# Preparation merged into the first attention: normalising, splitting and storing each pair of tiles while units run

## The reference

```python
x = x + _L0_xattn_ref(_layernorm(x, axis=-1), ctx_2048, ctx_2048)
# _L0_xattn_ref: 8 heads, each over 8 of the 64 rows of a batch
qk = jnp.einsum('bdm,bdn->bmn', qh, kh) * scale      # 256 x 256 for each head
sm = jax.nn.softmax(qk, axis=-1)
ret = jnp.einsum('bmn,bcn->bcm', sm, vh)
# _L3_xattn_ref: a decayed scan over the 64 context rows of a batch, then a mean over the rows,
# which the kernel folds into one weighted sum of the context's rows for each batch
```

## Time and profile before

| | |
|---|---|
| median of three runs | 2031.86 us (2029.39 to 2032.33) |
| span of the profiled execution | 2031.3 us; no other time is shown of that execution |
| busy: PE, DVE, ACT, POOL | 1408.2, 1363.5, 1120.5, 497.0 us |
| mean granted TensorE clock | 0.846 of full |
| preparation | 0 to 115.6 us (last store issued), first instruction behind the barrier at 118.9 |
| first attention | 118.9 to 579.2 us, with 64 units of about 6.3 us |
| DMA queue of SP | 116.46 MB, 23.0% of 16 engines' span |

### The profile page before, as it was taken

The page is one execution under the profiler, slowest core; times in us unless marked ns, Lnnn a source line. Parts: engine busy times, 40 slices in busy tenths (PEclk is TensorE's granted clock), DMA queues, the critical chain, the costliest instruction groups (busy, mean ns, idle before and its releaser), DMA issues. The chain is left out here.

```text
span 2031.3 us, 33248 instructions
## 1 busy us (share of the span) xinstructions
PE 1408.2 (69%) x11186; PEld 870.4 (43%) x11186; DVE 1363.5 (67%) x2850; ACT 1120.5 (55%) x1552; POOL 497.0 (24%) x903
## 2 busy tenths in 40 slices
PE   4429999999929894999626667379999646674111
PEld 4305555555527771555411333246565423342100
DVE  6646888888634534588867999535555468875896
ACT  4516777777712222677637888633434237875554
POOL 4411233333320004111013343200101001112663
PEclk9999999999959996999855766689999958877555
DMA  5652555555330003233110000011010120000111
GB/s 168 204 131 54 123 131 132 131 129 131 87 86 1 0 1 59 49 73 76 33 67 0 0 1 1 16 42 43 22 41 22 34 87 1 0 1 11 42 52 42
DMA packets 96387, 117.99 MB, mean 58 GB/s; under 512 B 29728, under 2 KB 82152, under 8 KB 91660
## 3 DMA queue, kind: packets, MB, share of 16 engines
q1 hardware_dynamic: 96268, 116.46, 23.0%
HBM read 80.07 MB, written 22.88 MB: 51 GB/s over the span
## 5 line engine op out<-in xcount | busy, mean ns | idle before, releaser
L610 DVE TENSOR_REDUCE ratt_nmax<-ratt_psS 128x2 f32<-128x512 f32 x512 | 318.7, 684 | 100.3 <-PE ratt_psS L502 98.7
L576 ACT ACTIVATE ratt_E<-ratt_psT 128x1024 f32<-128x1024 f32 x256 | 255.1, 1023 | 111.7 <-PE ratt_psT L524 111.6
L502 PE MATMUL ratt_psS<-ratt_K,ratt_Q 72*128 72x256 bf16 x1024 | 205.0, 285 | 42.9 <-DMA ratt_K<-context_parts 37.7
L524 PE MATMUL ratt_psT<-ratt_Q,ratt_K 75*128 75x256 bf16 x1024 | 196.8, 276 | 7.6 <-DMA ratt_Q<-ratt_rows 7.2
L502 PEld LDWEIGHTS ratt_psS<-ratt_K,ratt_Q 72*128 72x128 bf16 x1024 | 80.3, 99 | 139.5 <-issue 67.5
L537 PE MATMUL ratt_psO<-ratt_E,ratt_V 128*32 128x256 f32 x2048 | 138.8, 389 | 0.7 <-ACT ratt_E L576 0.7
L524 PEld LDWEIGHTS ratt_psT<-ratt_Q,ratt_K 75*128 75x128 bf16 x1024 | 99.9, 99 | 25.8 <-DMA ratt_Q<-ratt_rows 7.7
L3393 PE MATMUL final_psT<-final_identh,final_Z 128*128 128x128 f16 x64 | 8.3, 311 | 110.2 <-ACT final_Z L3427 110.2
L2195 PE MATMUL nffn_psH<-nffn_W,nffn_QT 128*128 128x512 bf16 x128 | 56.2, 589 | 28.8 <-ACT nffn_H L2274 19.9
L537 PEld LDWEIGHTS ratt_psO<-ratt_E,ratt_V 128*32 128x32 f32 x2048 | 53.8, 110 | 50.9 <-issue 28.1
L892 ACT COPY sffn_XS<-sffn_psG 128x512 f32<-128x512 f32 x8 | 4.7, 586 | 124.0 <-PE sffn_psG L841 124.0
(11 more groups left out here) (472 smaller groups left out, 3703.4 us busy)
## 6 DMA issues: line engine op xcount, KB each, us to landing
ratt_Q<-z_parts SPq DMA_DIRECT2D x32, 576.0 KB
ratt_K<-context_parts SPq DMA_DIRECT2D x96, 192.0 KB
gatt_V<-in_ctx_dram SPq DMA_DIRECT2D x16, 512.0 KB, 6.3
z_parts<-prep_ZS SPq DMA_DIRECT2D x48, 128.0 KB, 2.6
context_parts<-prep_CS SPq DMA_DIRECT2D x48, 128.0 KB, 2.3
head_sums<-ratt_O SPq DMA_DIRECT2D x64, 72.0 KB
all_X<-in_x_dram SPq DMA_DIRECT2D x8, 512.0 KB
prep_C<-in_ctx_dram SPq DMA_DIRECT2D x8, 512.0 KB
```

The source lines that it names most:

```text
L502: mm = nc.tensor.matmul(psS[:, RING[h], c * D:(c + 1) * D], Q9[0:R, buf, h, k % 2, c * P:(c + 1) * P], K9[0:R, buf, h, k % 2, :], start=Tr ...
L524: mm = nc.tensor.matmul(psT[:, p % 2, e, c, :], K9[0:RM, buf, h, u, c * P:(c + 1) * P], Q9[0:RM, buf, h, u, :], start=True, stop=True)
L576: nc.scalar.activation(E[:, 2 * b + p // 2, 2 * (p % 2):2 * (p % 2) + 2], psT[:, p % 2], ACT.Exp, scale=SCALE).then_inc(exped, 1)
L610: nc.vector.tensor_reduce(nmax[:, k % 2, h, :], psS[:, RING[h]].rearrange("p (c t) -> p c t", c=2), AX.X, ALU.max, negate=True).then_inc(m ...
```

## The change

Each engine does its steps of preparation at the end of its slot, behind everything of the units; the exceptions are `turn_context` on TensorE and `take_context` on ScalarE, which stand at the end of step p = 1:

```diff
+                # SP, behind bring_row, load_q or load_k, inverses_out, out, sums_back, back
+                    if at(n, 0) is not None:
+                        load_x(at(n, 0))
+                        load_c(at(n, 0))
+                    for part in range(3):
+                        if at(n, 3 + part) is not None:
+                            store_c(at(n, 3 + part), part)
+                        if at(n, 6 + part) is not None:
+                            store_z(at(n, 6 + part), part)
+                # load_q(g): sp.wait_ge(z_out, pair * 48 + 48); load_k(g): sp.wait_ge(c_out, pair * 48 + 48)
+                # TensorE, at the end of step p = 1
+                        if p == 1 and at(n, 1) is not None:
+                            turn_context(at(n, 1))
+                def turn_context(a):
+                    j = job["turn", a]
+                    pe.wait_ge(c_in[a % 2], a // 2 * 16 + 16)
+                    if j > 1:
+                        pe.wait_ge(exped, j - 1)
+                    for k in range(KC):
+                        for t in range(2):
+                            mm = nc.tensor.transpose(psT[:, j % 2, 0, k, t * P:(t + 1) * P],
+                                                     C[:, a % 2, t, k * P:(k + 1) * P], ident[:])
+                # ScalarE, behind the four exponentials (take_context at p = 1)
+                    if at(n, 2) is not None:
+                        first_of_c(at(n, 2))      # waits c_in, c_out of the pair before; copy to bf16
+                    if at(n, 4) is not None:
+                        normalise(at(n, 4))       # 2 activations, 128x256
+                    if at(n, 5) is not None:
+                        first_of_z(at(n, 5))      # waits z_out of the pair before; copy to bf16
+                # GpSimd, behind take, split_max, scale_and_add
+                    if at(n, 2) is not None:
+                        rest_of_c(at(n, 2))       # waits c_first of the same slot; subtract, 128x512
+                    if at(n, 3) is not None:
+                        root(at(n, 3))            # 4 small operations
+                        second_of_c(at(n, 3))     # copy to bf16, 128x512
+                    if at(n, 4) is not None:
+                        third_of_c(at(n, 4))      # subtract, 128x512
+                        weigh(at(n, 4))           # CT times the weights' row, 128x512
+                    if at(n, 6) is not None:
+                        rest_of_z(at(n, 6))       # subtract and copy to bf16, 128x512
+                    if at(n, 7) is not None:
+                        third_of_z(at(n, 7))      # subtract, 128x512
+                # VectorE, behind the maxima: take_stats (r = 1), aggregate (r = 2), sum_context (r = 6)
```

More of the change, by code:

```diff
@@ L427, in _ @@
[L427 to L434 removed]
+                        to = o_dram.rearrange("a (w g) c m -> a g c w m", g=4)[a, g]
@@ L475, in slot @@
-                def slot(i, k):
-                    n = i * 8 + k
+                    to = X[:, 2 * a:2 * a + 2, :]
+                    gp.tensor_tensor(to, to, num[:, a % 2], ALU.add).then_inc(added, 1)
+                for n in range(-LEAD, UNITS + 14):
                     if is_unit(n - LAG):
-                        take(i, k - LAG)
+                        take(n - LAG)
                     if is_unit(n - 1):
-                        split_max(n - 1, (k - 1) % 2)
-                    c = (k - 17) // 4
-                    if k % 4 == 1 and is_pair(i * 2 + c):
-                        scale_and_add(i * 2 + c, c % 2, i + c // 2)
@@ L485, in _ @@
-                slots(pool, slot, UNITS + 14)
+                        split_max(n - 1)
+                    if n % 4 == 1 and is_pair(n // 4 - 4):
+                        scale_and_add(n // 4 - 4)
+                    if at(n, 2) is not None:
[6 more added lines that the diff above has]
+                        weigh(at(n, 4))
@@ L562, in _ @@
-                slots(pe, slot, UNITS + LAG + 1)
+                            turn_max(n - 1)
             @block.scalar
             def _(act):
-                def row(u, b, half):
-                    act.wait_ge(turned, u + 1)
-                    if past(u, 2):
-                        act.wait_ge(row_in[b], half * 32)
-                    nc.scalar.copy(rows[:, b, :], psM[0:6 * NH0]).then_inc(row_out, 1)
-                def exp(m, b, p):
-                    act.wait_ge(shifted, m * 4 + (p + 1))
-                    if p == 0 and past(m, 2):
-                        act.wait_ge(pv, m - 1)
-                    nc.scalar.activation(E[:, 2 * b + p // 2, 2 * (p % 2):2 * (p % 2) + 2], psT[:, p % 2], ACT.Exp,
-                                         scale=SCALE).then_inc(exped, 1)
@@ new lines, in first_of_z, with first_of_c @@
+                def first_of_z(a):
+                    act.wait_ge(z_done, a * 2 + 2)
+                    if a > 0:
+                        act.wait_ge(z_out, a * 48)
+                    sc.copy(ZS[:, 0], Z[:]).then_inc(z_first, 1)
+                def first_of_c(a):
+                    act.wait_ge(c_in[a % 2], a // 2 * 16 + 16)
+                    if a > 0:
+                        act.wait_ge(c_out, a * 48)
+                    sc.copy(CS[:, 0], C[:, a % 2]).then_inc(c_first, 1)
+                act.wait_ge(decay_in, 16)
@@ L589, in slot @@
+                sc.activation(keep[:, 0:1], decay[:], ACT.Exp, scale=-1.0).then_inc(expd, 1)
+                for n in range(-LEAD, UNITS + LAG + 1):
                     m = n - LAG
@@ L613, in slot @@
[L613 to L622 removed]
+                            maximum(n, h)
```

683 lines of the change are left out of this document (322 added, 361 removed).

## The result

| | before | after |
|---|---|---|
| median of 4 runs | 2030.62 us (2029.39 to 2032.33) | 2093.69 us (2087.70 to 2094.44) |
| ratio to before | | 1.0307, 95% interval 1.0291 to 1.0323 |
| profiled execution, span | 2031.3 us | 2091.3 us (the run took 2093.05) |
| mean granted TensorE clock | 0.846 | 0.807 |
| copy of the row of unit 3, 8, 48, 63 (ACT) | 172.98, 203.75, 455.52, 549.66 | 68.36, 125.85, 504.51, 605.12 |

The account below looks back on a forecast made before the run. It took PE to be full (97.9 of 100 us) in the even attention, with no other engine near its limit. Span 2031.3 - 101 (front) + 129 (added to the slots) = 2059, so 2060 us, range 1992 to 2102.

Parts of the forecast that it names:

- The front: Start of the attention: first score at 40.5 us, slot 3 at 56 instead of 156.67, a gain of 101 us.
- The wait for C: TensorE's transposes wait for C, loaded too late in SP's queue: 5.9 us (4.9 to 7.8) per four slots.
- the list of the pairs: Which pairs wait for C: 5 to 15 in full, 11 times; pair 4 about 2 us; pair 3 none.
- GpSimd's chain: Remainder of C delays GpSimd's split for the turned maximum; TensorE waits 2.2 us (1.5 to 4.5) once in four slots.
- The transposes: Four f32 transposes of C added on TensorE per four slots: 0.9 us (0.45 to 1.0).
- The clock: TensorE's clock falls to 1.2 GHz behind the wait for C: 2.5 us per four slots (1 to 4).
- The third rival: The clock never comes back: slots of 8.5 us, 14.6 more per four slots, 2100 us; chance 0.17.
- The hidden edits: DVE's statistics and sum (0.7 us each) and ACT's copies and normalising (0.5 to 0.7 each) fit in idle time.
- the queues' order and not the busy time decides: Cost added to four slots: set by queue order, though SP's list holds 19 and GpSimd's 18 of 25 us.
- second rival: Everything hides, as busy shares suggest, if SP gets to the load early enough: 1943 us; chance 0.06.

Follow-up runs that it names:

- e10: Changed kernel with SP issuing x and C ahead of the inverses' and head sums' stores of the same slot; 2070.4 us, ratio 1.0185.
- e11: e7 with the loads of x and C put back into their slot of the changed kernel; 2076.3 us, ratio 1.0231.
- e1: Changed kernel with x and C loaded one slot earlier, pair 0 ahead of the loop; 2023.2 us, ratio 0.9957.
- e12: e7 with K loaded one slot earlier, and x and C two slots earlier than in the changed kernel; 1921.3 us, ratio 0.9464.
- e8: Changed kernel with 76 unused matmuls on TensorE ahead of its wait for C from pair 4 on; 2087.3 us, ratio 1.0265.
- e5: Kernel before with only the attention's loop written out slot by slot; 2035.6 us, ratio 1.0006.
- e2: Changed kernel with the load of C issued ahead of x instead of behind it; 2099.6 us, ratio 1.0321.
- e7: Changed kernel with x and C loaded one slot earlier, C's remainder one slot later, and a store semaphore for each part; 1966.7 us, ratio 0.9664.
- e3: Changed kernel with 56 unused matmuls on TensorE ahead of its wait for C in pairs 4 to 15; 2085.4 us, ratio 1.0276.

## Why the prediction was right in direction and wrong in size

**The front: right, by errors that cancel.** 101 us expected; slot 3 began 103.6 us earlier (its first shifted score at 53.08 for 156.67), and the row of unit 3 came 104.6 earlier. The first score came at 35.2 and not 40.5, 5.3 us better. Slots 0 to 2 took 17.9 us and not 15.5, of which 1.55 is a wait for pair 3's C where none was expected.

**The wait for C: the mechanism right, the size too small.** This is the step that failed. It was priced at 5.9 us: C issued at 11.7 and landing 3.3 later. Measured: issued 12.6 behind the slot's start, landing 4.0 later, a wait of 7.5. The 0.9 lie in SP's queue: from the first of the head sums to the issue of C the prediction had 3.3 us (2.8 for the sums, 0.5 for x), and it took 4.15, and 3.98 to 4.24 in all of the ten periods. The sums and x shared these differently each time (x's issue took 0.52 to 2.41 us), so that an x priced by itself, from a queue with nothing ahead of it, came out too cheap. The landing was within the stated bounds (2.3 to 5.2), and the whole within 4.9 to 7.8, at its upper end. e10 and e11 tie the wait to the load's place; e1 and e12 take it away.

The error also stood in the list of the pairs. Pair 4 waited 6.08 us and not 2, pair 5 8.38. The twelve waits of pairs 4 to 15 come to 89.0 us, where the prediction has 2 and eleven times 5.9, 66.9. These 22 us are the greater part of the 32 by which the span came out longer than forecast.

**GpSimd's chain: right in kind.** 2.2 expected, 1.55 measured, once in every period. The chain is as described: remainder of C at 359.80, the last part of the maximum at 364.25. The operations cost more than half of the old ones (1.155 for 1.06), but TensorE arrived later, because its clock was slow: with the clock at 1.00 in e8 the same wait took 2.45.

**The transposes.** 1.11 us for 0.9. In e12 the same four take 0.66, at full clock.

**The clock: right for the ordinary period, with some luck, and not for the rest.** 37.5 - 24.8 - 7.5 - 1.1 - 1.55 = 2.6, against 2.5, which had been picked between 1 and 4. But one of the ten periods took 42.7 us (from the transposes at 458.01 to those at 500.73), as the clock fell once more in its dense slots:
```profile
478.00:480.00 2.00, 1.37 (x17) 0.99 (x21) 0.88 (x2) 0.62 (x3) 1.68 (x7) 1.00 0.90 199
480.00:486.00 6.00, 6.00 (x45) 3.10 (x40) 3.64 (x6) 2.85 (x3) 5.41 (x11) 0.51 0.60 152
```
It fell behind the 1.55 us of the turned maximum here, and did not behind the same wait in the other nine. Pair 4's period (43.4 us, from 78.68 to 122.07), outside these ten, had the same second fall. The Trainium skill says that a kernel which waits for a DMA in each tile falls back to the cold clock each time ("TensorE: Matmul & The Clock Gate", HAM oscillation — how this bites in real kernels). The trace agrees: the granted clock fell to 0.50 at each of the twelve waits for C of pairs 4 to 15. The third rival, a clock that never comes back, did not hold: it was back at 353.8 in the period shown, 8 us behind the transposes, and within 6.4 to 12.3 in the others.

**What was added up wrongly.** Units 3 to 63 cost 160.1 more, for 129. Ten periods cost 12.7 each for 11.1 (16 in all). From unit 3 to 8 the cost was 26.7: this holds pair 4 and the wait and transposes of pair 5, for which the prediction has some 14. The last fifteen units cost 6.5 (100.6 us for 94.1). They hold the rest of pair 15's period, GpSimd's wait and most of its slow clock, some 4 in the prediction, and one more fall of the clock, at 538 us. The later stages took 4.5 more, which is within what the same code varies by, and the front gave 3.6 more.

**The hidden edits: hidden.** The unrolling costs nothing (e5). The statistics, the sum, the normalising and the splitting cost nothing once no load is late (e12). The prediction's sentence that the queues' order and not the busy time decides was borne out more than the sum used it. Its second rival, that everything hides once SP gets to the load early enough, was given 0.06 and a time of 1943. It is what the same work does once x and C are issued two slots earlier, K and the remainder of C stand in other slots and each store has its own semaphore: 1921.

**What stays open.** Why the clock falls behind one wait of 1.55 us and not behind the next was not settled. The traces of the changed kernel and of e2 show a sign that goes with it. Behind nine of their 24 waits for C (pairs 4 to 15) the clock stayed low for 11.3 to 12.7 us from the transposes on, and all nine times it fell again behind the turned maximum; the other fifteen times it stayed low for 6.4 to 8.5 us and did not fall again. In e10 one fall (386.5 us) breaks this pattern. What decides how long it stays low was not tried.

## What to carry to other kernels

When work is folded into the slots of a full engine, its price is not its busy time but the place of its loads in the queue. For each load, put down the slot in which the queue can issue it, what stands ahead of it, the landing time under load, and the slot in which it is wanted; if the last is not later than the sum, move the issue by whole slots. A reshuffle in the slot shortened the wait by 0.85 us (e2) or 2.6 (e10), where a whole slot took it away.

Cure the waits together. Short waits left over (1.3 to 3 us) often brought the slow clock back and cost about twice their own length: from e7 to e12 the period fell by 3.9 us for 1.7 of waiting for K. The wait for the turned maximum of 1.55 us brought it back in only two of twelve periods of the changed kernel. One cure at a time makes each look small, as the waits hide one another.

Ahead of filling a wait with idle work, ask which wait comes next: e8 filled it wholly and gained 6 us.

## What the runs showed of the hardware

- A granted clock of 1.00 fell to 0.50 behind waits of 1.3 to 3.0 us (e3: 1.34 us of wait ended at 379.93, 0.67 in the next window, then 0.50; e1: 3.02), and stayed there for some 4 (e8) to 10 us (e1) of full work. In the kernel before, with no wait above 0.8 us, it was 1.00 from 200 to 500.
- SP's issue of 256 KB took 0.41 to 0.59 us with little ahead of it (e10, e12) and 1.67 and 1.08 behind the four stores of head sums, which took 2.39 themselves. From the first of these stores to the issue of C it was 3.98 to 4.24 us in ten periods, though the stores took anything from 1.48 to 3.46.
- Stores of 128 KB, which landed in 2.3 us in the old preparation, took 4.7 (C) and 5.0 (Z) over the changed kernel, whose DMA share was 0.50 from 150 to 450, and 6.2 and 4.8 in e12, at a share of 0.67, where no wait of TensorE came of it.
- A 128x512 subtraction of GpSimd took 1.155 us, a little more than half of the 2.12 of twice the size, its cast 0.61.
